# One decoder layer over 16 blocks of tokens on one core: the four hand-written instruction orders of the attention half rearranged

## The reference

```
x = x + latent(layernorm(x))     # width 64, compressed to 32; one head, causal, rotary
x = x + cross(layernorm(x), ctx) # 32 heads of 8 in 8 groups (4 query heads share a key head), causal
x = x + experts(layernorm(x))    # 32 experts, top 8 softmax gates cut at a cumulated share of 0.8
```

## Time and profile before

| | |
|---|---|
| median of 3 timed runs | 516.5 us |
| the three runs | 511.64, 516.5, 516.7 us |
| the execution that was profiled | 512.39 us |
| its span, first to last instruction | 510.5 us |
| PE, DVE, ACT, POOL busy in the span | 454.5, 378.2, 317.9, 327.5 us |
| granted TensorE clock, mean | 0.983 |

### The profile page before, as it was taken

The page is one execution under the profiler, slowest core; times in us unless marked ns, Lnnn a source line. Parts: engine busy times, 40 slices in busy tenths (PEclk is TensorE's granted clock), DMA queues, the critical chain, the costliest instruction groups (busy, mean ns, idle before and its releaser), DMA issues.

```text
span 510.5 us, 12310 instructions
## 1 busy us (share of the span) xinstructions
PE 454.5 (89%) x3120; PEld 389.1 (76%) x3120; DVE 378.2 (74%) x1854; ACT 317.9 (62%) x869; POOL 327.5 (64%) x473
## 2 busy tenths in 40 slices
PE   3689999999999999999978999989999999999920
PEld 2467787787787787777756998879999999888910
DVE  4356788888877888877896885655565667999886
ACT  2477778777778777778735555556565656555520
POOL 4112167777767777777667777777676767665770
PEclk9999999999999999999999999999999999999985
DMA  6331447862232232322128679999655679998785
GB/s 191 110 133 54 166 141 207 232 175 87 95 104 93 94 116 79 104 92 76 62 87 257 200 251 312 294 295 290 209 156 147 203 216 316 339 351 305 256 276 178
DMA packets 52261, 93.79 MB, mean 184 GB/s; under 512 B 9974, under 2 KB 41246, under 8 KB 52002
## 3 DMA queue, kind: packets, MB, share of 16 engines
q1 hardware_dynamic: 37346, 46.11, 31.2%
q0 software_dynamic: 12240, 32.14, 16.8%
q10 hardware_dynamic: 2608, 14.76, 8.7%
HBM read 53.61 MB, written 43.41 MB: 190 GB/s over the span
## 4 chain that ended last, share of the span: by engine, by line
PE 52%; DVE 21%; DMA 8%; issue 6%; ACT 5%; SPq 4%; POOL 2%; POOLq 0%; ACTq 0%; DVEq 0%
PE bank L1411 11%; PE bank L1443 7%; DVE NM L789 7%; PE bank L1104 5%; DVE NM L791 4%; PE bank L1362 4%; PE bank L1245 4%; PE bank L1287 3%; PE bank L1261 3%; DMA qN<-rows 2%; PE bank L1433 2%; PE bank L1166 2%; SPq L361 2%; PE bank L1099 2%; DMA KA<-parts 2%
## 5 line engine op out<-in xcount | busy, mean ns | idle before, releaser
L469 POOL DMA_INDIRECT rows<-rowb,idx x112 | 110.8, 989 | 55.1 <-DVE rowb L889 28.4
L1411 PE MATMUL bank<-wgu_sb,PT 128*128 x572 | 105.0, 327 | 0.7 <-ACT PT L496 0.7
L1411 PEld LDWEIGHTS bank<-wgu_sb,PT 128*128 128x128 f32 x572 | 91.3, 190 | 0.8 <-issue 0.8
L479 POOL DMA_INDIRECT parts<-PT,dst_all x72 | 71.4, 991 | 29.4 <-issue 21.9
L496 ACT ACTIVATE PT<-bank 128x512 f32<-128x512 f32 x108 | 61.4, 593 | 28.1 <-PE bank L1443 19.3
L1443 PE MATMUL bank<-wd_sb,VC 96*128 x286 | 73.6, 379 | 0.0
L589 ACT ACTIVATE PT<-bank 128x512 f32<-128x512 f32 x96 | 53.7, 621 | 4.7 <-PE bank L1261 4.6
L1443 PEld LDWEIGHTS bank<-wd_sb,VC 96*128 96x128 f32 x286 | 52.2, 190 | 4.0
L998 DVE SCALAR_TENSOR_TENSOR PT<-PT,bank 128x192 f32<-128x192 f32 x72 | 25.2, 350 | 40.0 <-ACT PT L623 39.8
L623 ACT ACTIVATE PT<-bank 128x192 f32<-128x192 f32 x72 | 23.7, 329 | 45.2 <-PE bank L1411 45.2
L496 ACT ACTIVATE Q<-bank 9x256 fp32r<-9x256 f32 (+1 forms) x96 | 42.5, 443 | 11.3 <-PE bank L1240 9.6
(11 more groups left out here) (270 smaller groups left out, 1141.8 us busy)
## 6 DMA issues: line engine op xcount, KB each, us to landing
pool_a<-rows SPq DMA_DIRECT2D x96, 148.5 KB
qN<-rows SPq DMA_DIRECT2D x47, 148.5 KB
wgu_sb<-wgu_d SPq DMA_DIRECT2D x8, 768.0 KB, 4.9
rows<-pad SPq DMA_DIRECT2D x33, 152.0 KB
pool_a<-parts ACTq DMA_DIRECT2D x5, 896.0 KB, 6.5
KA<-parts ACTq DMA_DIRECT2D x5, 896.0 KB
Q<-parts ACTq DMA_DIRECT2D x5, 896.0 KB, 7.0
wd_sb<-wd_d SPq DMA_DIRECT2D x2, 1536.0 KB
```

Of the source, the lines that this page charges most:

```text
L469: gp.indirect_dma_start(out=rows, out_offset=bass.IndirectOffsetOnAxis(ap=idx[b % 2][:, k:k + 1], axis=0), in_=rowb[b % 2][:, :], in_offse ...
L479: gp.indirect_dma_start(out=parts, out_offset=bass.IndirectOffsetOnAxis(ap=dst[q % NDST][:, j:j + 1], axis=0), in_=yb[q % FEED][:, j, :], ...
L1411: last = t.matmul(GU_PS[q % 2][:, j * 2 * NI:(j + 1) * 2 * NI], xTb[q % 2][:, j, k * P:(k + 1) * P], wgu_sb[:, k, one_of(expert[i]), :].sq ...
```

## The change

The change moves steps in the four tables, splits two steps, and takes one step's PSUM from the ring.

- **Early latent products.** `r7` and `r8` go earlier on PE, ACT, DVE and POOL: on PE `r7` stands ahead of `lg`, `r8` right behind `pv1`; on DVE `r7` stands right behind `r1`; on POOL it moves from behind `sc1` and `xT` to between `sc0` and `sc1`. `r12` goes ahead of `kT` on PE and on ACT (where `kT` is the eight key copies), and `r13` ahead of `c` on PE.
- **Second query half in a ring bank.** `r17b` takes the next ring bank and no longer waits for ACT's copy of the first half; ACT reads it from there.
- **Value transposes between the query halves.** On PE: `r17`, `vt`, `r17b`, `kv`, `r9`, `rk`.
- **Key copies ahead of the latent exponential.** ACT's `kv` is split: the key copy stays `kv`, the value copies become `kva` and wait for DVE's `klo`. Both stand right ahead of `r10`, behind `r8` and both query copies (before, all copies stood ahead of `r8`). The bank is now given back by the value copies.
- **DVE.** `po` is split: the product with the rank stays ahead of `mx0`, the other two instructions become `px`. `px`, `g5`, `g6`, `g7` move behind the maxima: `... mx5 r10 wo r4 r13 n3 g5 g6 r5 px g7 g8 ... g13`, where it was `... mx5 r10 wo r4 r13 r5 g8 g9 n3 g10 ... g13`.
- **SP.** `n3` moves behind `ldx`; in particular that of block 1 stands behind `ldx` of block 4.
- In the last blocks `g5` and `g6` come to stand behind `vt` of the next block (before: ahead of it); the rest keeps its order there.

The diff without the table entries:

```
-READ = {"kv": ("klo", 1), ...
+READ = {"r17b": ("Q2", 2), "kv": ("va", 1), ...
...
-                    copy(Q2[b % 2][0:CR, hf, :, :, :], R_PS[b % 2][0:CR, :].rearrange(...)).then_inc(S["Q2"], 1)
+                    o = ring_bank("r17b", b) if hf else R_PS[b % 2]
+                    copy(Q2[b % 2][0:CR, hf, :, :, :], o[0:CR, :].rearrange(...)).then_inc(S["Q2"], 1)
...
-                copy(kN3[b % 2][:, :, 0:3:2, :], o[:, 0:GD]...)
+                copy(kN3[b % 2][:, :, 0:3:2, :], o[:, 0:GD]...).then_inc(S["kh"], 1)
+
+            def kva(b):
+                o = ring_bank("kv", b)
+                act.wait_ge(S["klo"], nth("klo", b))
...
             def kv(b):
-                dve.wait_ge(S["va"], nth("va", b))
+                dve.wait_ge(S["kh"], nth("kh", b))
...
                 v.tensor_tensor(pt[:, :], ring_bank("rk", b)[:, 0:NE], M16[b % 2][:, :], ALU.mult).then_inc(S["pt"], 1)
+
+            def px(b):
                 dve.wait_ge(S["pt"], nth("pt", b))
                 v.max(rowb[b % 2][:, D + NE:D + NE + TOP], pt[:, :]).then_inc(S["p8"], 1)
...
-                    else:
-                        pe.wait_ge(S["Q2"], nth("Q2", b, 1))
+                    o = ring("r17b", b) if hf else R_PS[b % 2]
                     for h in range(HG):
-                        last = t.matmul(R_PS[b % 2][0:CR, h * P:(h + 1) * P], ...
+                        last = t.matmul(o[0:CR, h * P:(h + 1) * P], ...
```

More of the change, by code:

```diff
@@ L54 @@
 AT = {
[2 rows of a table removed]
[2 rows of a table added]
            "c": 32.9, "sm": 34.4, "s0": 34.5, "s1": 35.6, "s2": 36.1, "s3": 36.6, "s4": 36.8, "s5": 37.6, "pv0": 38.9, "pv1": 40.2,
-           "vt": 43.5, "oT": 46.6, "wo": 50.8, "xT": 56.9, "lg": 58.0, "rk": 62.9, "la1": 74.5 + (SEEN - 1) * PERIOD,
+           "vt": 42.46, "oT": 48, "wo": 50.8, "xT": 56.9, "lg": 58.0, "rk": 62.9, "la1": 74.5 + (SEEN - 1) * PERIOD,
            "la2": 80 + (SEEN - 1) * PERIOD, "la3": 87.8 + (SEEN - 1) * PERIOD},
[4 rows of a table removed]
[4 rows of a table added]
            "wqc": 17, "r16": 22.2, "mx0": 27.9, "mx1": 28.6, "mx2": 29.3, "mx3": 30.2, "mx4": 31, "mx5": 31.5,
[1 row of a table removed]
-           "po": 62.9, "g7": 64, "g8": 73.7, "g9": 74.2, "g10": 75.2, "g11": 75.4, "g12": 75.6, "g13": 75.8, "la1": 77.4 + (SEEN - 1) * PERIOD,
[1 row of a table added]
+           "po": 62.9, "px": 72.6, "g7": 73, "g8": 73.7, "g9": 74.2, "g10": 75.2, "g11": 75.4, "g12": 75.6, "g13": 75.8, "la1": 77.4 + (SEEN - 1) * PERIOD,
            "la2": 83 + (SEEN - 1) * PERIOD, "la3": 88.2 + (SEEN - 1) * PERIOD},
-    "POOL": {"r1": -12, "r4": -2.2, "r7": 3.9, "r13": 17.4, "kL": 29.5, "r17": 46.3, "wo": 51.5, "xT": 60, "sc0": 74.6, "sc1": 77.4, "sc2": 80.5,
+    "POOL": {"r1": -12, "r4": -2.2, "r7": 2.3, "r13": 17.4, "kL": 29.5, "r17": 46.3, "wo": 51.5, "xT": 60, "sc0": 74.6, "sc1": 77.4, "sc2": 80.5,
            "sc3": 82.6, "sc4": 84.5, "sc5": 86.4, "sc6": 87.7},
-    "SP": {"ldx": -6.0, "ldc": -2.0, "n3": 42.5, **{f"w{n}": 25.0 + 12.0 * n for n in range(10)}}}
+    "SP": {"ldx": -6.0, "ldc": -2.0, "n3": 54, **{f"w{n}": 25.0 + 12.0 * n for n in range(10)}}}
 ONCE = {"mi", "mk", "wqs", "wqc", "la1", "la2", "la3"} | {f"w{n}" for n in range(10)}
 PAIR0, PAIR = 47.1, 3.2
-SOON = {"g7": (0, -1.2, 0), **{f"g{n}": (-6, -10.6, -12.5) for n in range(8, 14)}, **{f"sc{k}": (-5, -9.26 + 1.1 * k - (0, 2.8, 5.9, 8, 9.9, 11.8, 13.1)[k], -11 + 1.1 * k - (0, 2.8, 5.9, 8, 9.9, 11.8, 13.1)[k]) for k in range(SENT)}}
+SOON = {"n3": (0, 2.1, 0), "g5": (-10.6, -10.6, 0), "g6": (-10.35, -10.35, 0), "px": (-9.65, -9.65, 0), "g7": (-9, -10.2, 0), **{f"g{n}": (-6, -10.6, -12.5) for n in range(8, 14)}, **{f"sc{k}": (-5, -9.26 + 1.1 * k - (0, 2.8, 5.9, 8, 9.9, 11.8, 13.1)[k], -11 + 1.1 * k - (0, 2.8, 5.9, 8, 9.9, 11.8, 13.1)[k]) for k in range(SENT)}}
 END = {
@@ L76 @@
     "ACT": {"oT": 47.3, "xT": 53.6, "g1": 57},
-    "DVE": {"wo": 50.6, "n3": 52.2, "g1": 56.9, "g2": 57.9, "g3": 58, "g4": 58.1, "g5": 58.2, "po": 60.3, "g6": 61, "g7": 61.1},
+    "DVE": {"wo": 50.6, "n3": 52.2, "g1": 56.9, "g2": 57.9, "g3": 58, "g4": 58.1, "g5": 58.2, "po": 60.3, "px": 60.35, "g6": 61, "g7": 61.1},
     "POOL": {"r17": 28.5, "wo": 48.4}}
@@ L98 @@
 ENDING = [(s, NB - 1) for s in ("oT", "wo", "xT", "lg", "rk")]
-READ = {"kv": ("klo", 1), "kT": ("KA", 1), **{f"mx{u}": ("rmax", u + 1) for u in range(6)}, "c": ("Q3c", 2),
+READ = {"r17b": ("Q2", 2), "kv": ("va", 1), "kT": ("KA", 1), **{f"mx{u}": ("rmax", u + 1) for u in range(6)}, "c": ("Q3c", 2),
         **{f"s{i}": ("e", i + 1) for i in range(6)}, "vt": ("on", 1),
@@ L546, in f @@
                         act.wait_ge(S["s"], nth("s", b - 2, 6))
-                    copy(Q2[b % 2][0:CR, hf, :, :, :], R_PS[b % 2][0:CR, :].rearrange("p (h a n) -> p a h n", h=HG, a=2)).then_inc(S["Q2"], 1)
+                    o = ring_bank("r17b", b) if hf else R_PS[b % 2]
+                    copy(Q2[b % 2][0:CR, hf, :, :, :], o[0:CR, :].rearrange("p (h a n) -> p a h n", h=HG, a=2)).then_inc(S["Q2"], 1)
                 return f
@@ L674, in _ @@
                       "mk": mk, "r7": r7, "r8": r8, "r10": r10, "r11": r11, "r12": r12, "r15": r15, "r16": r16, "r17": q_rows(0), "r17b": q_rows(1),
-                      "kv": kv, "kT": kT, "c": c, **{f"s{i}": s_(i) for i in range(6)}, "pv1": pv,
+                      "kv": kv, "kva": kva, "kT": kT, "c": c, **{f"s{i}": s_(i) for i in range(6)}, "pv1": pv,
                       "oT": oT_, "xT": xT, "g1": g1})
@@ L1189, in f @@
                         pe.wait_ge(S["ql"], nth("ql", b))
-                    else:
-                        pe.wait_ge(S["Q2"], nth("Q2", b, 1))
+                    o = ring("r17b", b) if hf else R_PS[b % 2]
                     for h in range(HG):
-                        last = t.matmul(R_PS[b % 2][0:CR, h * P:(h + 1) * P], qN[b % 2][:, 2 * h + hf, :, :].rearrange("p a c -> p (a c)"), identr[:, :], start=True, stop=True)
+                        last = t.matmul(o[0:CR, h * P:(h + 1) * P], qN[b % 2][:, 2 * h + hf, :, :].rearrange("p a c -> p (a c)"), identr[:, :], start=True, stop=True)
                     last.then_inc(S["qT"], 1)
```

4 lines of the change are left out of this document (2 added, 2 removed), and 16 rows, old and new, of tables (AT, names).

## The result

The changed kernel is slower. Its median is 520.88 us (4 runs, 516.68 to 522.53) against 514.07 us of the kernel before (4 runs, 509.72 to 516.7). The ratio is 1.013, with a 95% interval of 1.0075 to 1.0189. I had forecast 509 us, with 0.05 for slower.

A forecast was written before the change was run, and what follows sets the result against it. A loop of POOL and DVE waiting for each other sets part of the 15.31 us period. Start -1.6, next two periods -2.6, eleven periods -2.5, the 16.48 period -1.4, last blocks +0.8: -7.3, so 509 us; range 501 to 515.5.

The forecast's parts named there:

- DVE's share: DVE from `r5` to the end of `g13`: 1.87 us becomes 2.19; `n3` leaves, `px` and `g7` come in.
- The loop: POOL and DVE waiting for each other: period 15.1 us against 15.31, ends 15.0 and 15.4.
- the five cases: The forecast itself, given a chance of 0.53, and the four numbered rivals.
- PE's waits ahead of `r9` and `c`: Sign of a right forecast: PE's waits of 0.25 and 0.24 us a period disappear.
- The wait ahead of `r7` for `chT`: Sign of a right forecast: PE, its own loop at about 14.7 us, waits here instead; no size given.
- Start: First block 1.6 us less (ends 0.5 and 2.2); the next two periods 2.6 less (ends 1.5 and 3).
- The 16.48 period (-1.4): Period ending at 245.43: with `g5` behind the maxima it becomes like the others, 1.4 us less.
- the 0.8 of the last blocks: `g5` and `g6` of blocks 13 and 14, now behind `vt`, add 0.3 and 0.5 us on DVE's path.
- (3): Rival: on POOL the rope sum blocks the scatters when PE's `r7` is late; slower, 520 us; chance 0.07.
- (2): Rival: POOL holds DVE's moved sums 0.55 us a period; loop 15.65, total 515.7 us; chance 0.10.
- (1): Rival: loop not shortened, 15.33 a period, since `n3` holds POOL and the rope-sum gap stays; 512 us; chance 0.20.
- (4): Rival: PE sets the pace at 14.7 us a period, POOL's loop having slack; 504.5 us; chance 0.10.

The follow-up runs named there:

- run 2: Changed kernel with three row buffers in place of two, nothing else: 507.2 us, ratio 0.987 to the kernel before.
- run 4: Kernel before with SP's `n3` alone moved behind `ldx`: 513.37 us, one run, so no ratio.
- run 6: Changed kernel with three row buffers, and `g5` and `g6` of the last blocks ahead of `vt` again: 505.94 us, ratio 0.985 to the kernel before.
- run 7: Changed kernel, two row buffers, with `g5`, `g6`, `px`, `g7` back ahead of the maxima, `n3` left ahead of `r5`: 519.88 us, ratio 1.014 to the kernel before.
- run 11: Changed kernel, two row buffers, with `n3` back behind `g9` and `g5`, `g6`, `px`, `g7` back ahead of the maxima: 515.06 us, ratio 1.001.
- run 5: Changed kernel with three row buffers, and `px` and `g7` ahead of `r5` on DVE: 504.83 us, ratio 0.983 to the kernel before.
- run 9: Changed kernel, two row buffers, with `g5`, `g6`, `px`, `g7` ahead of `n3` and `r5` on DVE: 507.77 us, ratio 0.986 to the kernel before.
- run 10: Changed kernel with three row buffers, `px` and `g7` ahead of `r5`, and last blocks' `g5` and `g6` ahead of `vt`: 503.87 us, ratio 0.978.

## Why the prediction was wrong

**The step that failed** is the first clause of *DVE's share*, "`n3` leaves", with the ends of *The loop*, where I priced the new place of `n3` by one thing only, that it "runs beside POOL's 1/std and could hold it". I never asked what `n3` itself waits for. Its second wait never appears as idle time in the trace of before, so that a list of waits could not show it; the code and the times of the seventh scatter and of `n3` could have. None of the five cases had this mechanism, and the step put it at nothing. What the runs showed in its place: DVE stands about 0.8 us a period for the landing at `n3`, all of `g5` to `g13` and the first scatter stand behind it, and the loop is 15.6 instead of 15.1. That is about 0.5 us a period, and it goes with a third buffer (run 2).

**The loop that I did see was sized rightly**, which run 2 shows, where the other is gone: from the first scatter to the end of the 1/std for `r5` 11.9 us (forecast 12.0), from `r5` to the end of `g13` 2.18 (2.19), period 15.06 (15.1). For that kernel the medians differ by 514.67 - 507.2 = 7.5, where the forecast was 7.3, but that nearness is partly luck: by the traces its first expert product starts at 270.31, 5.1 us earlier than before (0.5 to block 0, 2.2 in the next two periods, 3.0 in the eleven, less 0.6 in the last two), and the profiled run gives 2.3 of that back in the second half (237.49 for 235.17). Where the medians have the rest from is not known; the executions differ there anyway. The rope sum no longer waits on POOL, and PE's waits ahead of `r9` and `c` are gone, as forecast, in run 2 and in the changed kernel too, where the loop through the landing takes the gain. The wait ahead of `r7` for `chT` shows on PEld alone, 0.4 us at most in the changed kernel.

**Start.** -1.2 and -2.2 for -1.6 and -2.6. The way to the maxima of block 0 differs from execution to execution by up to 2 us: it takes 29.4 to 30.2 us in the profiles with the old start and 28.1 to 30.2 in those with the new one, so the -1.2 is not clear of it. The two periods are firm: 28.6 to 29.2 in all nine profiles with the new order. They got 0.6 and 1.6 shorter, where the forecast had 0.7 and 1.9, of which 1.2 for SP's move; run 4 does not tell that part from the differences between executions.

**The 16.48 period (-1.4).** It does become like the others once the landing is out of the way (15.11 in run 2), but the next one pays it back: 18.44 for 16.54 before. `g5`, `g6`, `px` and `g7` of block 12 pass behind the maxima of block 14, while those of block 13 stay ahead of block 15's, so that this period has both. DVE is busy 16.13 us of it in run 2, 14.03 before. I had counted the gain where the steps left, and at the place where they arrive only 0.8 for `g5` and `g6`. Over both periods run 2 is 0.6 slower than before (33.55 for 32.94). Two readings of mine were a little off beside this: in DVE's order of time the period behind block 7's maxima is 15.20, not the 15.12 of the chain, which still is less than 15.31; and the range's lower end, 512 less 12, is 500 and not 501.

**The end of the changed kernel** (+3.2 in the period from block 12 to 13, +4.2 behind block 14) was in none of my terms, but for the 0.8 of the last blocks. In run 2, with nobody at the landing, the first is gone (15.06) and 1.9 of the second is left, so most of it comes with the wait for the landing. The landings grow there; the chain has them at these places:

```profile
201.44 3.02 DMA rows<-rowb,idx
...
217.56 3.68 DMA rows<-rowb,idx
...
234.81 4.65 DMA rows<-rowb,idx
```

Behind the second of them PE waits 1.69 us at `r6`, and a microsecond later its clock is at half. PE's order of time, and the busy times of 223 to 227 us (the last columns are granted clock, DMA share and GB/s):

```profile
222.37 0.28 PE L1141 MATMUL bank<-con,chat 128*32 128x128 f32 x1 [1.69 <-DVE chat L700]
...
223.38 1.97 PE L1111 MATMUL bank<-wq_sb,pool_a 128*128 128x256 f32 x4
```
```profile
223.00:227.00 4.00, 4.00 (x26) 2.98 (x22) 2.64 (x16) 1.64 (x4) 1.35 (x2) 0.57 0.09 38
```

The same four products take 1.13 us at 112.29, at 2.4 GHz. The granted clock is at 1.2 GHz for 3.41 us there, for 3.41 from 257.7 and for 6.83 from 267.9. The period of 18.48 is close to 15.57, the usual one, with 1.2 for the longer landing (3.68 for 2.48) and 1.7 for half of 3.41 us. That this clock is the price of PE's waits is my reading; no run tested it. For it: no other profile has a wait of this length at `r6`, or a fall of the clock between 39 and 254 us. Against it: PE waits 1.63 us in the kernel before and 2.33 in run 6 at the end of the first half, and 1.43 at 240.6 in the changed kernel itself, with no fall behind it. Why the landings grow is open too; the wait for them is not the reason, since in run 2, where nobody waits, those of 197.96, 212.96 and 228.06 take 3.3, 3.3 and 3.6 us, where in the kernel before they take 2.5 up to that of 217.96.

**The rivals.** (3) has nearly the measured time, 520, and (2) the measured period, 15.65, both by coincidence: neither of their mechanisms is in the changed kernel's repeating blocks. (1), the loop not shortened, is right in that the period did not fall, for a reason that it did not give. (2), sums of DVE held by POOL, is absent there: the moved sums at 126.42, beside a 1/std of POOL (126.11 for 0.55), and at 127.22 take 0.17 and 0.18; but runs 7 and 11 show it at the place that the sums had before, at 0.58 us a period, close to the 0.55 that I gave it elsewhere. The Trainium skill, SBUF — State Buffer, section "Who interferes with whom", has it that a DVE instruction with two SBUF inputs and a GpSimd instruction that reads SBUF exclude each other for the whole of one. The trace agrees beside POOL's 0.73 us add and not beside its 1/std, where the sum takes its usual 0.16. (3) is out: the rope sum waits for nobody in the changed kernel, nor in run 2. (4) is out in the changed kernel, and near in runs 5, 9 and 10, where periods of 14.8 are reached once both loops are shortened.

## What to carry to other kernels

Before you move an instruction ahead, list every semaphore that it waits for and read in the trace when each arrives, the ones that never show as a wait first: the distance between arrival and start is the margin that the move spends. A wait for a buffer to be free closes a loop through whatever empties it, here seven scatters and a landing, and all that stands behind the wait in the engine's order is added to that loop; so put the independent work ahead of the wait (here run 9, 1.4%), or add a buffer (run 2, 1.3%). And when a step leaves one period for the next, find the period at the end that gets two of them.

## What was not expected of the hardware

The landing of the seventh scatter took 2.5 us from the start of the scatter in the middle of the first half and 3.0 to 4.7 at its end, while the DMA engines were busy for 0.50 of the time during the landing of 2.48 from 123.25, for 0.54 during that of 3.68 and for 0.20 during that of 4.65, so that their load does not tell the lengths apart. A DVE sum over 128x8 elements took 0.73 to 0.75 us instead of 0.15 when it started 0.02 to 0.05 us behind a POOL add over 128x256, and ended with it; in four cases of run 7, all at a distance of 0.02 us or less, it took 0.15, so that a few hundredths of a us decide over 0.58 us a period.

A scatter's own row on POOL, by which I had read the loop, is 0.96 us long, so the landing lies 1.5 us behind its end and shows only in the chain and in a wait. The Trainium skill, Perfetto Trace Analysis, section "DMA Instruction — SWDGE (GPSIMD)", says that such a row ends when the descriptors are written and not when the data has moved; the trace agrees (0.96 beside 2.48). By the Trainium skill, DMA: Bandwidth & Descriptors, section "Anatomy of one DMA — SWDGE (gpsimd) path", an estimate for a buffer of 128 rows of 304 float32 is 2.4 us (2.0 and the bytes by 436 GB/s): the landings of 2.46 and 2.48 agree, those of 3.0 to 4.7 do not.
